# Four-head attention of a two-layer kernel: six weighing rounds of a query tile become five, the sixteenth key tile's values go in three column pieces, and the last piece of the exponents' sum, now of four tiles, is added on VectorE

## The reference, cut to what matters

```python
Q = (nx @ Wq.T).reshape(B, S, H, dk).transpose(0, 2, 1, 3)     # H = 4, dk = 32
Kc = nx @ Wkc.T
Vc = nx @ Wvc.T
scores = jnp.einsum('bhsd,btd->bhst', Q, Kc) * scale
attn = jax.nn.softmax(scores, axis=-1)
out = jnp.einsum('bhst,btd->bhsd', attn, Vc)
out = out.transpose(0, 2, 1, 3).reshape(B, S, d) @ Wo.T
```

## Time and profile before

| | |
|---|---|
| median of 3 runs | 643.61 us (642.26 to 643.88) |
| the profiled execution, its own time | 642.2 us |
| its span, first to last instruction | 640.5 us |
| TensorE busy | 593.0 us, 93% of the span |
| VectorE busy | 469.1 us, 73% |
| GpSimd busy | 369.8 us, 58% |
| ScalarE busy | 353.0 us, 55% |
| granted TensorE clock, mean | 0.991 of full speed |

### The profile page before, as it was taken

One profiled execution on the slowest core, in us unless ns is written; L12 is line 12 of the kernel. 1 busy time (PEld: TensorE's weight loads), 2 busy tenths in 40 slices (PEclk: granted clock), 3 DMA queues, 4 the chain that ended last, 5 costly groups with the idle time before them and its releaser, 6 DMA issues.

```text
span 640.5 us, 12614 instructions
## 1 busy us (share of the span) xinstructions
PE 593.0 (93%) x4528; PEld 398.6 (62%) x4529; DVE 469.1 (73%) x1097; ACT 353.0 (55%) x710; POOL 369.8 (58%) x420
## 2 busy tenths in 40 slices
PE   4888899899989899969999999999999999999996
PEld 2566799767655566645555554555555543788885
DVE  5767344449968778898777778777777775788986
ACT  2645455436854555525677776866676656442222
POOL 6607400177548433707888887898788879415220
PEclk9999999999999999988999999999999999999999
DMA  9801122120000000000000000000000000000101
GB/s 285 358 2 47 55 67 66 37 54 10 0 1 3 2 3 2 3 2 1 1 1 1 2 1 2 2 0 1 2 1 1 1 1 1 2 1 2 34 1 34
DMA packets 16617, 17.34 MB, mean 27 GB/s; under 512 B 1712, under 2 KB 15024, under 8 KB 16176
## 3 DMA queue, kind: packets, MB, share of 16 engines
q1 hardware_dynamic: 15536, 14.49, 6.8%
q0 software_dynamic: 1024, 2.10, 1.1%
HBM read 11.34 MB, written 5.24 MB: 26 GB/s over the span
## 4 chain that ended last, share of the span: by engine, by line
PE 71%; DVE 12%; POOL 6%; issue 4%; ACT 4%; DMA 3%; SPq 0%; DVEq 0%; ACTq 0%; POOLq 0%
PE ps L2078 12%; PE ps L2068 10%; PE ps L2058 8%; PE ps L2206 5%; DVE region L1116 3%; PE ps L1881 3%; PE ps L1788 3%; PE ps L1771 3%; PE ps L2196 2%; PE ps L2198 2%; PE ps L2197 2%; POOL slots_in L628 2%; PE ps L1969 2%; DMA region<-slots_in 2%; PE ps L1871 2%
## 5 line engine op out<-in xcount | busy, mean ns | idle before, releaser
L1116 DVE TENSOR_REDUCE region<-ps 128x1 f32<-128x512 f32 x256 | 161.1, 684 | 54.3 <-PE ps L2058 53.8
L1561 ACT ACTIVATE region<-ps 128x512 f32<-128x512 f32 x256 | 138.0, 598 | 54.5 <-PE ps L2068 54.2
L775 POOL TENSOR_TENSOR region<-region 128x512 f32<-128x512 f32 x80 | 107.1, 1342 | 26.2 <-ACT region L1561 23.4
L2068 PE MATMUL ps<-qmr,kr 98*128 98x512 f32 x256 | 112.0, 442 | 1.5 <-ACT region L1561 0.8
L2058 PE MATMUL ps<-kr,qmr 96*128 96x512 f32 x256 | 102.4, 410 | 1.7 <-DVE region L1116 0.9
L2078 PE MATMUL ps<-region 128*32 128x512 f32 x512 | 91.8, 599 | 0.0
L2085 PE MATMUL ps<-region,ones 128*32 128x512 f32 x192 | 91.6, 599 | 0.2 <-DVE region L1132 0.2
L780 POOL TENSOR_TENSOR region<-region 128x512 f32<-128x512 f32 x64 | 81.9, 1279 | 12.2 <-ACT region L1561 8.2
L2068 PEld LDWEIGHTS ps<-qmr,kr 98*128 98x128 f32 x256 | 48.8, 192 | 53.6 <-issue 24.7
L2058 PEld LDWEIGHTS ps<-kr,qmr 96*128 96x128 f32 x256 | 49.4, 194 | 13.8 <-DVE region L1116 7.0
L1665 ACT ACTIVATE region<-ps 128x512 f32<-128x512 f32 x36 | 21.5, 598 | 56.8 <-PE ps L2198 56.8
(11 more groups left out here) (286 smaller groups left out, 1189.9 us busy)
## 6 DMA issues: line engine op xcount, KB each, us to landing
region<-in_w SPq DMA_DIRECT2D x2, 2048.0 KB, 13.0
slots_in<-zeros SPq DMA_DIRECT2D x1, 1536.0 KB, 8.7
region<-slots_in SPq DMA_DIRECT2D x6, 256.0 KB, 2.8
slots_out<-og SPq DMA_DIRECT2D x6, 256.0 KB, 2.4
e<-in_e SPq DMA_DIRECT2D x1, 1152.0 KB, 15.5
x<-in_x SPq DMA_DIRECT2D x4, 256.0 KB, 3.9
out<-y SPq DMA_DIRECT2D x3, 256.0 KB, 2.3
e<-in_e SPq DMA_DIRECT2D x1, 576.0 KB, 16.7
```

Source lines behind the costliest of these rows:

```text
L775: ins = pool.tensor_tensor(o, held(tiles[0]), held(tiles[1]), ALU.add)
L1116: dve.tensor_reduce(mxp[:, u // HM, u % HM:u % HM + 1], bank(b), AX.X, ALU.max).then_inc(mx_read, 1)
L1561: act.activation(pm[:, t // 2, t % 2 * HM * P:(t % 2 + 1) * HM * P], bank(SCORE_BANKS[n % 3]), ACT.Exp, scale=SCM).then_inc(p_whole, 1)
L2068: pe.matmul(bank(SCORE_BANKS[n % 3]), kr[0:M_ROWS, t * P:(t + 1) * P], rows_of(i)[0:M_ROWS, :], start=True, stop=True).then_inc(st_filled, 1)
```

## The change

`ROUNDS` has five rounds, the last of tiles 12, 13, 14 and 15, and `PIECES` is the same list. In the last round three matmuls of 512 columns take the values of tiles 12 to 14 as before, one matmul of ones takes the sum of all four tiles, and the values of tile 15 are taken by three short matmuls of 171, 171 and 170 columns, one in each of the groups 0 to 2. GpSimd has four pieces of three tiles, two adds each. VectorE has the fifth piece in three dependent adds: two behind its maximum of slot 15, one behind that of slot 17. The buffers of `sp` are taken in turn over all query tiles.

```diff
-ROUNDS = [(0, 1, 2), (3, 4, 5), (6, 7, 8), (9, 10, 11), (12, 13, 14), (15,)]
-PIECES = [(0, 1), (2, 3, 4), (5, 6, 7), (8, 9, 10), (11, 12, 13), (14, 15)]
+ROUNDS = [(0, 1, 2), (3, 4, 5), (6, 7, 8), (9, 10, 11), (12, 13, 14, 15)]
+PIECES = ROUNDS
+SPREAD = (0, 171, 342, 512)
-ROUND_SLOT = (8, 8, 14, 14, 19, 19)
+ROUND_SLOT = (8, 8, 14, 14, 19)
...
             def whole_sum(i, p, first):
...
-                o = sp[:, p % SUM_RING, :]
+                o = sp[:, (i * NR + p) % SUM_RING, :]
...
-                ins = pool.tensor_tensor(o, held(tiles[0]), held(tiles[1]), ALU.add)
-                if len(tiles) == 3:
-                    ins.then_inc(sum_step, 1)
-                    pool.wait_ge(sum_step, i * (POOL_PIECES - 1) + p)
-                    pool.wait_ge(p_whole, i * NT + tiles[2] + 1)
-                    ins = pool.tensor_tensor(o, o, held(tiles[2]), ALU.add)
-                ins.then_inc(sum_ready, 1)
+                pool.tensor_tensor(o, held(tiles[0]), held(tiles[1]), ALU.add).then_inc(sum_step, 1)
+                pool.wait_ge(sum_step, i * POOL_PIECES + p + 1)
+                pool.wait_ge(p_whole, i * NT + tiles[2] + 1)
+                pool.tensor_tensor(o, o, held(tiles[2]), ALU.add).then_inc(sum_ready, 1)
...
-            def last_sum(i):
-
-                dve.wait_ge(round_done, i * NR + NR - SUM_RING)
-                dve.wait_ge(p_whole, i * NT + NT)
-                dve.tensor_tensor(sp[:, (NR - 1) % SUM_RING, :], pm[:, (PAIRS - 1) % HELD, 0:HM * P],
-                                  pm[:, (PAIRS - 1) % HELD, HM * P:2 * HM * P], ALU.add).then_inc(last_sum_ready, 1)
+            def last_pieces(i, n):
+
+                o = sp[:, (i * NR + NR - 1) % SUM_RING, :]
...
+                if n == 0:
+                    dve.wait_ge(round_done, i * NR + NR - SUM_RING)
+                    dve.wait_ge(p_whole, i * NT + b + 1)
+                    dve.tensor_tensor(o, held(a), held(b), ALU.add).then_inc(last_step, 1)
+                elif n == 1:
+                    dve.wait_ge(last_step, 2 * i + 1)
+                    dve.wait_ge(p_whole, i * NT + c + 1)
+                    dve.tensor_tensor(o, o, held(c), ALU.add).then_inc(last_step, 1)
+                else:
+                    dve.wait_ge(last_step, 2 * i + 2)
+                    dve.wait_ge(p_whole, i * NT + d + 1)
+                    dve.tensor_tensor(o, o, held(d), ALU.add).then_inc(last_sum_ready, 1)
...
                     if t == 1 and not first:
-                        last_sum(i - 1)
+                        last_pieces(i - 1, 2)
...
+                    if t == NT - 1:
+                        last_pieces(i, 0)
+                        last_pieces(i, 1)
...
-            last_sum(NT - 1)
+            last_pieces(NT - 1, 2)
...
-                for t in ROUNDS[r]:
+                for t in ROUNDS[r][0:PARTS]:
...
-                pe.matmul(bank(6)[DM * PARTS:P, :], ones[:, 0:DM], sp[:, r % SUM_RING, :], start=(r == 0), stop=(r == NR - 1),
-                          skip_group_check=True).then_inc(round_done, 1)
+                ins = pe.matmul(bank(6)[DM * PARTS:P, :], ones[:, 0:DM], sp[:, (i * NR + r) % SUM_RING, :], start=(r == 0), stop=(r == NR - 1),
+                                skip_group_check=True)
+                for t in ROUNDS[r][PARTS:]:
+                    for g in range(PARTS):
+                        a, b = SPREAD[g], SPREAD[g + 1]
+                        ins = pe.matmul(bank(6)[DM * g:DM * (g + 1), a:b], qkv[:, t, D + DM:D + 2 * DM],
+                                        pm[:, t // 2 % HELD, t % 2 * HM * P + a:t % 2 * HM * P + b],
+                                        start=False, stop=True, skip_group_check=True)
+                ins.then_inc(round_done, 1)
```

More of the change, by code:

```diff
@@ L390, in bass_recurrent_two_layers @@
         tile_ready = sem("tile_ready"); q_turned = sem("q_turned"); qm_ready = sem("qm_ready")
-        sum_step = sem("sum_step"); sum_ready = sem("sum_ready"); last_sum_ready = sem("last_sum_ready"); oT_ready = sem("oT_ready"); o_turned = sem("o_turned")
+        sum_step = sem("sum_step"); last_step = sem("last_step"); sum_ready = sem("sum_ready"); last_sum_ready = sem("last_sum_ready"); oT_ready = sem("oT_ready"); o_turned = sem("o_turned")
         mr_ready = sem("mr_ready"); st_filled = sem("st_filled"); p_whole = sem("p_whole"); round_done = sem("round_done")
@@ L769, in whole_sum @@
                 tiles = PIECES[p]
-                o = sp[:, p % SUM_RING, :]
+                o = sp[:, (i * NR + p) % SUM_RING, :]
                 held = lambda t: pm[:, t // 2 % HELD, t % 2 * HM * P:(t % 2 + 1) * HM * P]
-                if not (first and p < SUM_RING):
+                if i * NR + p >= SUM_RING:
                     pool.wait_ge(round_done, i * NR + p - SUM_RING + 1)
                 pool.wait_ge(p_whole, i * NT + tiles[1] + 1)
-                ins = pool.tensor_tensor(o, held(tiles[0]), held(tiles[1]), ALU.add)
-                if len(tiles) == 3:
-                    ins.then_inc(sum_step, 1)
-                    pool.wait_ge(sum_step, i * (POOL_PIECES - 1) + p)
-                    pool.wait_ge(p_whole, i * NT + tiles[2] + 1)
-                    ins = pool.tensor_tensor(o, o, held(tiles[2]), ALU.add)
-                ins.then_inc(sum_ready, 1)
+                pool.tensor_tensor(o, held(tiles[0]), held(tiles[1]), ALU.add).then_inc(sum_step, 1)
+                pool.wait_ge(sum_step, i * POOL_PIECES + p + 1)
+                pool.wait_ge(p_whole, i * NT + tiles[2] + 1)
+                pool.tensor_tensor(o, o, held(tiles[2]), ALU.add).then_inc(sum_ready, 1)
             cross_added(NG - 1)
@@ L1126, in high_maximum @@
                 dve.tensor_copy(qtile2[:, parity, :, R_ROWS].bitcast(F32R), negm[:, :]).then_inc(m_step, 1)
-            def last_sum(i):
-                dve.wait_ge(round_done, i * NR + NR - SUM_RING)
-                dve.wait_ge(p_whole, i * NT + NT)
-                dve.tensor_tensor(sp[:, (NR - 1) % SUM_RING, :], pm[:, (PAIRS - 1) % HELD, 0:HM * P],
-                                  pm[:, (PAIRS - 1) % HELD, HM * P:2 * HM * P], ALU.add).then_inc(last_sum_ready, 1)
+            def last_pieces(i, n):
+                o = sp[:, (i * NR + NR - 1) % SUM_RING, :]
+                held = lambda t: pm[:, t // 2 % HELD, t % 2 * HM * P:(t % 2 + 1) * HM * P]
+                a, b, c, d = PIECES[-1]
+                if n == 0:
[10 more added lines that the diff above has]
+                    dve.tensor_tensor(o, o, held(d), ALU.add).then_inc(last_sum_ready, 1)
             def shared_out(i):
@@ L2079, in weigh @@
                               pm[:, t // 2 % HELD, t % 2 * HM * P:(t % 2 + 1) * HM * P],
-                              start=(t < PARTS), stop=(t + PARTS >= NT), skip_group_check=True)
+                              start=(t < PARTS), stop=False, skip_group_check=True)
                 if r < POOL_PIECES:
```

## The result

The changed kernel takes 661.02 us (median of 4 runs, 659.73 to 662.07), the kernel before on the same chip 642.93 (4 runs, 640.34 to 643.88). The ratio is 1.028, with a 95% interval of 1.025 to 1.030: 18.1 us slower. The forecast was 661.0.

A forecast was written before the change was run, and what follows sets the result against it. The prediction took TensorE to bound the kernel, with VectorE falling behind in slots 15 to 19. It summed 13.2 + 4.6 + 1.6 - 0.5 = +18.9 us on 642.2, 661.1, said 661; its own range 655 to 667, 8-in-10 range 649 to 667.

The forecast's parts named there:

- The first two adds between two maxima: Slots 15 to 20: VectorE's adds delay slot 20 by 1.40 us in five plain places, 0.69 in nine with preparation; +13.2 us.
- The meeting with GpSimd: Slots 15 to 20: VectorE's and GpSimd's adds make each other stand still; 0.31 us a place, inside the +13.2.
- GpSimd's later pieces: Slots 8 and 11: pieces end a key tile later; six tiles lose 0.45 us, three 0.40, five 0.13; +4.6 us.
- The moment of `round_done`: Last round: its signal, now on the last short matmul, comes with the end of the ones, as today; no gain taken.
- The short matmuls: Tile 15's values on TensorE: 0.36 us a tile side by side against 0.88 for the round, so TensorE alone gains 0.52.
- The end: Last piece of the last tile: all three adds stand before its ones, 0.79 + 0.79 more, nothing to hide it; +1.6 us.
- The bounds of 0 and of a whole GpSimd add: Slots 15 to 20: limits for the price of VectorE's adds meeting GpSimd's, between 0 and 1.28 us a tile.

The follow-up runs named there:

- The first experiment: Changed kernel with VectorE's first two adds of the last piece at slot 14, ahead of slot 15's maximum (early adds): ratio 0.9965 to the kernel before, 661.8 us against 664.7.
- the third experiment: Kernel before, six rounds kept, with two dependent VectorE adds more, into their own buffer, behind the maximum of slot 15: ratio 1.029 to the kernel before.
- the reductions: Changed kernel with each of VectorE's three adds replaced by a one-operand reduction with the same waits: ratio 1.017 to the kernel before.
- two left out: Changed kernel with only VectorE's add of tiles 14 and 15 left, behind slot 17's maximum; tiles 12 and 13 left out of the sum: ratio 0.9971 to the kernel before.
- one early: Changed kernel with VectorE's first add at slot 14, the second still behind slot 15's maximum: one run, slot 20 at 5.53 us after slot 15 in 13 of 14 places.
- GpSimd's old pieces and late adds: Changed kernel with GpSimd's pieces (0, 1), (2, 3, 4), (5, 6, 7), (8, 9, 10) and its add of 11 and 12; VectorE's adds not moved early: ratio 1.0204 to before.
- early adds and GpSimd's old pieces: Changed kernel, VectorE's first two adds early, GpSimd's pieces (0, 1), (2, 3, 4), (5, 6, 7), (8, 9, 10) and its add of 11 and 12: ratio 1.0066 to before.

## Why the prediction was right

The order of events was right: VectorE late, TensorE's piece of slot 19 waiting for it, the ones waiting for the third add, `turn_maxima` waiting for `low_maximum`. That 661 meets the median of 661.02 so closely is luck. The sum was +18.9 us on an execution of 642.2, which is 661.1; carried to the median of the runs shown, 1.4 us higher, it would have been 662.5, and the prediction gives no reason for leaving that out. Measured are +18.1 by the medians. In the profiles the terms that were forecast come to 12.5 + 4.4 + 0.6 = 17.5, and one of them is right only through a cancellation, as told below.

**The first two adds between two maxima** (+13.2 us forecast). Right. Slot 20 was to begin at 5.98 with and without preparation; it begins at 5.97 to 5.98 in 12 of the 14 places. Against before the 14 places lost 12.5 us: 1.40 in each plain one, 0.69 in seven with preparation, and 0.43 and 0.31 in tiles 1 and 14, where fewer things meet. The first experiment shows it by moving the adds, the third by adding them to the kernel before.

**The meeting with GpSimd** (0.31 a place in that sum). Right, 0.38 by the reductions in 12 places. The two lengths behind it hold as well: above, the third add ends 0.55 us after GpSimd's L776 (0.56 in the prediction's rows).

**GpSimd's later pieces** (+4.6). Right in size: the 14 tiles lost 16.9 - 12.5 = 4.4 us outside slots 15 to 20, and GpSimd's old pieces give 4.5 back. In the six tiles forecast at 0.45, `turn_maxima` starts 6.83 to 6.84 after slot 20 (6.81 forecast). Elsewhere the parts were off and made up for each other: the five tiles forecast at 0.13 lost 0.2 and one of them 0.35, since slot 8 lost 0.20 and not 0.13, and tiles 6 and 10 nothing and not 0.40, since what slot 11 lost there came back before slot 15.

**The moment of `round_done`**. The short matmuls' records end at 449.91; ScalarE's copy, which waits for the last of them, starts at 450.55, 0.16 after slot 20 (0.11 before):

```profile
450.55 0.60 ACT L1581 ACTIVATE region<-ps 128x512 f32<-128x512 f32 x1 [2.65 <-PE ps L2102]
```

So the short matmul's signal came with the end of the ones ahead of it: the copy starts 0.09 after the end of the ones' record (450.46) in all 14 places, and about 0.6 after that of the short ones. With early adds, in places with preparation, the short ones end last, and the copy starts 0.06 after their record. This agrees with what the Trainium skill says (TensorE: Matmul & The Clock Gate, section "The mechanism"), that matmuls end in program order.

**The short matmuls** (0.36 us for all six passes). A little less: where TensorE waits for no one, in tile 15, slot 20 begins at 3.38 instead of 3.96. That is 0.58 saved, 0.52 forecast, so that of the round's 0.88 the short ones take 0.30.

**The end** (+1.6). This term was wrong, and a cancellation hid it. It took the three adds to start where the one add started before, 1.79 us after slot 15 of the last tile, with two pairs of 0.79 behind it. But that moment is not fixed: VectorE was done with its other work earlier there. Its first two adds are over 0.1 us after slot 15 began (563.72), and the third waits for nothing but the exponents of tile 15:

```profile
563.12 0.69 DVE L1138 TENSOR_TENSOR region<-region 128x512 f32<-128x512 f32 x1
564.96 0.69 DVE L1142 TENSOR_TENSOR region<-region 128x512 f32<-128x512 f32 x1 [1.14 <-ACT region L1573]
```

So from slot 15 to the next stage's first matmul the kernel took 2.96 us and not the 3.50 before: 0.5 less where 1.6 more was forecast. Slots 20 to 31, forecast to stay as they were, took 1.7 more (12.79 and not 11.09). Part of that is a stretch at the lower clock, after one with gaps on TensorE:

```profile
560.00:564.00 4.00, 4.00 (x21) 1.20 (x19) 3.71 (x9) 0.79 (x2) 3.48 (x4) 0.62 0.01 4
564.00:570.00 6.00, 5.51 (x31) 3.06 (x31) 3.15 (x11) 3.66 (x6) 3.54 (x1) 1.00 0.00 0
```

The experiments tell the two apart. The four that keep the changed kernel's pieces on GpSimd (early adds, two left out, reductions, one early) had the full clock in the last tile, and all of them took 2.95 to 2.96 at the end and 11.7 for slots 20 to 31. So the short end does not come from the clock, 0.6 of the 1.7 comes from the pieces, and 1.1 is seen only together with the lower clock. With GpSimd's old pieces and late adds the first add starts at 0.69 and the end takes 3.86, even there only 0.4 more than before. What brought the lower clock in this one execution was not tried. All in all tile 15 and the end cost 0.6 us and not 1.1; without the stretch at the lower clock it would have been about -0.5, and the sum 1.1 us further off.

The bounds of 0 and of a whole GpSimd add were both too wide to be of use; what carried the forecast was a timetable of eight instructions with durations from rows.

## What to carry to other kernels

An engine with 25% idle time can still be late for everyone: before giving it work, write out the ten instructions around the place, with the number of buffers between it and the engine that waits. A saving on the bounding engine is real only if the work that pays for it stands in a gap and not behind an instruction that someone waits for; here the same two adds 2 us earlier turned 2.8% slower into 0.35% faster, and GpSimd's old pieces, a third add one slot earlier and two GpSimd instructions moved out of that gap, all three together, made it 0.9%. When an add on VectorE and one on GpSimd both read two tiles, plan them as one queue.

## What the runs showed of the hardware that I had not expected

- After a wait of 1.15 us on TensorE, amid other gaps, the granted clock fell to 0.51 for 3 us in one tile of the third experiment, while the waits of 1.0 us in the changed kernel's plain places did not lower it. In the run with early adds and GpSimd's old pieces it was at 0.50 for 10 us after a wait of 1.18 us, at the same place. Which part of the stretch counted is open.
- A difference of some 20 us between chips lay wholly ahead of the attention. Parts of a query tile that no edit touched took the same time on all four chips: slots 20 to 24 of tile 2 took 2.42 to 2.44 us in all eleven profiles.
- A cast of 128 x 4 elements on VectorE, 0.17 us at its shortest, took 0.52 in the median before and 1.12 after. In 15 of its 16 executions, before as after, a GpSimd add ran beside it, and it ended 0.03 us after that add, here at 455.67 against 455.64. VectorE, then GpSimd, in the profile after:

```profile
454.55 1.12 DVE L1124 CAST region<-region 128x4 fp32r<-128x4 f32 x1
```
```profile
454.37 1.27 POOL L776 TENSOR_TENSOR region<-region 128x512 f32<-128x512 f32 x1
```

  So not only VectorE's two-input adds stand still behind GpSimd: this cast reads one operand and writes four columns. VectorE had nothing urgent behind the cast, and it cost no time here.
